# A linear-attention phase of a fused transformer kernel: a new step order, a three-pass output projection, and q's squares on another engine

## The reference

```
q, k, v = silu(x@Wq), silu(x@Wk), silu(x@Wv)          # 16 heads x 64
g = sigmoid(x@Wf - dt_bias); beta = sigmoid(x@Wb); A = exp(-exp(A_log))
q, k = q/|q|, k/|k|
for t:  o_t = (q_t . state) * g_t
        state = A*state + beta_t * k_t (x) v_t
o = o * rsqrt(mean(o*o) + 1e-5) * norm_w * sigmoid(x@Wg + bg)
y = o @ Wo                                            # 1024 -> 128
```

## Time and profile before

| | us |
|---|---|
| median of 3 runs | 917.35 (914.67 to 918.21) |
| the profiled execution | 915.93 |
| its span | 913.8 |

### The profile page before, as it was taken

The page is one execution under the profiler, slowest core; times in us unless marked ns, Lnnn a source line. Parts: engine busy times, 40 slices in busy tenths (PEclk is TensorE's granted clock), DMA queues, the critical chain, the costliest instruction groups (busy, mean ns, idle before and its releaser), DMA issues. The chain is left out here.

```text
span 913.8 us, 31013 instructions
## 1 busy us (share of the span) xinstructions
PE 841.7 (92%) x13152; PEld 717.5 (79%) x13152; DVE 548.9 (60%) x1247; ACT 511.6 (56%) x1105; POOL 636.4 (70%) x530
## 2 busy tenths in 40 slices
PE   4858998999797789999999999999999999998897
PEld 3648998899695678887888888888888888877786
DVE  3986566566684455655655655656556556666563
ACT  4745553565566636645646556566466467364354
POOL 3973211321455988898898898898898898988352
PEclk9998999999997889999999999999999999999999
DMA  5001000100100000000000000000000000000011
GB/s 189 25 13 34 25 12 1 31 19 1 25 1 1 1 3 3 3 3 3 3 3 2 3 4 2 3 4 2 3 3 3 4 2 3 4 1 3 3 36 57
DMA packets 19415, 12.36 MB, mean 14 GB/s; under 512 B 7760, under 2 KB 18768, under 8 KB 19024
## 3 DMA queue, kind: packets, MB, share of 16 engines
q1 hardware_dynamic: 19280, 10.39, 3.9%
HBM read 8.29 MB, written 2.10 MB: 11 GB/s over the span
## 5 line engine op out<-in xcount | busy, mean ns | idle before, releaser
L2101 POOL TENSOR_TENSOR la_scale<-la_scale,lt_mhalf 128x32 f32<-128x32 f32 x16 | 100.6, 6285 | 43.4 <-DVE la_scale L1756 43.4
L1446 PE MATMUL la_ps<-la_x_hi,w_hi 128*128 128x256 f32 x384 | 120.2, 313 | 0.4 <-ACT la_v L1897 0.4
L1447 PE MATMUL la_ps<-la_x_lo,w_hi 128*128 128x256 f32 x384 | 108.2, 282 | 0.0
L1448 PE MATMUL la_ps<-la_x_hi,w_lo 128*128 128x256 f32 x384 | 108.1, 281 | 0.0
L2061 POOL TENSOR_TENSOR la_coef<-la_ssk,lt_mhalf 128x32 f32<-128x32 f32 x16 | 87.0, 5440 | 13.8 <-DVE la_ssk L1774 13.8
L1797 DVE TENSOR_TENSOR lt_state<-la_s_ps,la_faded 128x512 f32<-128x512 f32 x62 | 42.3, 682 | 71.9 <-PE la_o_ps L1525 48.6
L1446 PEld LDWEIGHTS la_ps<-la_x_hi,w_hi 128*128 128x128 f32 x384 | 72.9, 190 | 16.0 <-issue 7.4
L531 POOL CAST at_q_hi<-qk_hi 128x128 fp32r<-128x128 f32 x32 | 9.4, 294 | 106.1 <-PE at_s_ps L572 103.6
L598 PE MATMUL at_o_ps<-V,at_probsT 128*128 128x128 f32 x544 | 75.1, 278 | 3.2 <-DVE at_probsT L507 2.0
L2079 POOL TENSOR_TENSOR la_k<-la_k,lt_decay_k 128x1024 f32<-128x1024 f32 x32 | 75.6, 2364 | 2.1 <-ACT n_xn L1953 2.1
L2086 POOL TENSOR_TENSOR la_qdT<-la_qT,lt_decay_q 128x1024 f32<-128x1024 f32 x32 | 76.3, 2384 | 0.0
(11 more groups left out here) (207 smaller groups left out, 2382.6 us busy)
## 6 DMA issues: line engine op xcount, KB each, us to landing
at_w_raw<-in_w SPq DMA_DIRECT2D x20, 128.0 KB, 2.2
X<-in_x SPq DMA_DIRECT2D x8, 256.0 KB, 2.9
out<-X SPq DMA_DIRECT2D x8, 256.0 KB, 2.3
qkv_cos<-in_cos SPq DMA_DIRECT2D x1, 1024.0 KB, 4.8
qkv_sin<-in_sin SPq DMA_DIRECT2D x1, 1024.0 KB, 7.0
lt_w_out<-in_w_out SPq DMA_DIRECT2D x4, 128.0 KB, 2.7
const<-in_const SPq DMA_DIRECT2D x1, 320.5 KB, 3.2
qkv_w<-in_w_qkv SPq DMA_DIRECT2D x1, 320.0 KB, 3.9
```

Of the source, the lines that this page charges most:

```text
L1446: eng.matmul(out, l_hi, r_hi, start=True, stop=False)
L1447: eng.matmul(out, l_hi, r_lo, start=False, stop=False)
L1448: return eng.matmul(out, l_lo, r_hi, start=False, stop=True)
L2101: eng.tensor_tensor(scale[:, :, :], scale[:, :, :], powers, ALU.pow).then_inc(s["scale_step"], 1)
```

## The change

- **Order.** Every engine's step is rearranged. On TensorE the whole-array products are put together, and the quarter-array work between them stands in five groups: su; then attend, turn_k, attend, recall; scores, sq, recall, update; attend, turn_k, attend, recall; scores, recall, update. The scores of the first sequence are made one step earlier (`scored`), as is `fade(m, 0, 0)`. `turn_scales` and the b jobs come after the first update, `project_out` after q3.
- **Projection.** ScalarE copies u to a high part (`high_u`), VectorE makes the low part (`low_u`), and `project_out` runs three fp32r products for each of 8 chunks. The weights are split once, in the lead-in. To make room, u_hi and u_lo lie on the memory of sq and gate and the weights' low part on that of w_out, with waits added for it.
- **q's squares** go from VectorE to ScalarE (`square_q`), and **one of two `decay_queries`** from GpSimd to VectorE.

```diff
-def make_room(self, sb):
+def make_room(self, nc, sb):
+    with ExitStack() as whole:
+        self.w_out = whole.enter_context(nc.sbuf_tensor("lt_w_out", [P, NP, P], F32))
+    self.w_out_lo = sb("lt_w_out_lo", [P, NP, P], F32R)
+    self.w_out_hi = sb("lt_w_out_hi", [P, NP, P], F32R)
...
 faded = sb("faded", [P, B, NP, D])
 u = sb("u", [P, NP, W])
-sq = sb("sq", [P, NP, W])
+with ExitStack() as before_scaling:
+    sq = before_scaling.enter_context(nc.sbuf_tensor("la_sq", [P, NP, W], F32))
+    gate = before_scaling.enter_context(nc.sbuf_tensor("la_gate", [P, NP, W], F32))
+u_hi = sb("u_hi", [P, NP, W], F32R)
+u_lo = sb("u_lo", [P, NP, W], F32R)
...
-        return exists(m + 1) if job != "sq" else exists(m)
+    if job in ("be", "s00", "s01") or job[0] in "kqv":
+        return exists(m + 1)
     return exists(m)
 STEPS = range(-2, NT + 1)
 LAST = NT - 1
-ring = Ring(("f0 be s00 s01 f1 su k0 f2 sT k1 f3 v0 kT0 kT1 sq g0 k2 g1 k3 g2 sB g3 v1 b0 b1 b2 b3 v2 y s10 s11 "
-             "v3 yt xt q0 q1 kT2 kT3 q2 q3").split(), has, STEPS, BANKS)
+ring = Ring(("f0 f1 su f2 sT f3 be k0 k1 v0 v1 kT0 kT1 k2 k3 s10 s11 sq sB b0 b1 b2 b3 v2 v3 q0 q1 q2 q3 y g0 g1 yt g2 "
+             "kT2 kT3 g3 xt s00 s01").split(), has, STEPS, BANKS)
+def scored(m, b):
+    return m - 1 if b == 0 else m
 def free(eng, m, job):
...
-    for job in ("kT2", "kT3", "q3"):
-        taken(eng, m - 1, job)
-banks = [free(eng, m, f"s{b}{odd}") for odd in range(2)]
+for job in ("kT2", "kT3") if b else ("kT0", "kT1", "q3"):
...
-    for j in range(4):
-        taken(eng, m, f"b{j}")
+    if m == 1:
+        eng.wait_ge(s["w_lo_ready"], 1)
+    eng.wait_ge(s["ulo_ready"], 4 * m)
     bank = free(eng, m, "y")
+    out = ps[bank][:, 0:W]
     for c in range(NP):
-        mm = eng.matmul(ps[bank][:, 0:W], w_out[:, c, :], u[:, c, :], start=(c == 0), stop=(c == NP - 1))
+        eng.matmul(out, tables.w_out_hi[:, c, :], u_hi[:, c, :], start=(c == 0), stop=False)
+        eng.matmul(out, tables.w_out_hi[:, c, :], u_lo[:, c, :], start=False, stop=False)
+        mm = eng.matmul(out, tables.w_out_lo[:, c, :], u_hi[:, c, :], start=False, stop=(c == NP - 1))
     mm.then_inc(full[bank], 1)
 def turn_y(m):
...
     prv, now, nxt = exists(m - 1), exists(m), exists(m + 1)
     if now:
         by_feature(m, "f0")
-    if nxt:
-        betas(m + 1)
-    if now:
-        scores(m, 0)
-    if now:
         by_feature(m, "f1")
     if prv:
         sum_squares(m, "su")
-    if nxt:
-        by_token(m, "k0")
     if now:
         by_feature(m, "f2")
     if prv:
         turn_totals(m)
-    if nxt:
-        by_token(m, "k1")
     if now:
         by_feature(m, "f3")
     if nxt:
+        betas(m + 1)
+        by_token(m, "k0")
+        by_token(m, "k1")
         by_token(m, "v0")
-        turn_k(m, 0)
-    if now:
-        sum_squares(m, "sq")
-        by_feature(m, "g0")
-    if nxt:
-        by_token(m, "k2")
-    if now:
-        by_feature(m, "g1")
-    if nxt:
-        by_token(m, "k3")
-    if now:
-        by_feature(m, "g2")
-    if prv:
-        turn_scales(m)
-    if now:
-        by_feature(m, "g3")
-    if nxt:
         by_token(m, "v1")
-    if prv:
-        for j in range(4):
-            spread_scales(m, j)
     if now:
         attend(m, 0, 0)
     if nxt:
-        by_token(m, "v2")
+        turn_k(m, 0)
     if now:
         attend(m, 0, 1)
-    if m == 0:
-        update((m, 0, 0))
-    if prv:
-        project_out(m)
+        recall(m, 0, 0)
+    if nxt:
+        by_token(m, "k2")
+        by_token(m, "k3")
     if now:
-        recall(m, 0, 0)
         scores(m, 1)
-    if nxt:
-        by_token(m, "v3")
-    if prv:
-        turn_y(m)
-    if m == LAST:
-        eng.wait_ge(up_read[1], B * LAST)
-        ffn.turn(eng, 0)
-    if exists(m + 2):
-        turn_x(m + 2)
-    if now:
+        sum_squares(m, "sq")
         recall(m, 0, 1)
     if now and nxt:
         update((m, 0, 1), (m, 1, 0))
     elif now:
         update((m, 1, 0))
+    if prv:
+        turn_scales(m)
+        for j in range(4):
+            spread_scales(m, j)
+    if m == LAST:
+        eng.wait_ge(up_read[1], B * LAST)
+        ffn.turn(eng, 0)
     if nxt:
-        by_feature(m, "q0")
-        by_feature(m, "q1")
+        by_token(m, "v2")
+        by_token(m, "v3")
+        for j in range(4):
+            by_feature(m, f"q{j}")
+    if prv:
+        project_out(m)
     if now:
+        by_feature(m, "g0")
+        by_feature(m, "g1")
+    if prv:
+        turn_y(m)
+    if now:
+        by_feature(m, "g2")
         attend(m, 1, 0)
     if nxt:
         turn_k(m, 1)
     if now:
         attend(m, 1, 1)
+        recall(m, 1, 0)
+        by_feature(m, "g3")
+    if exists(m + 2):
+        turn_x(m + 2)
+    if nxt:
+        scores(m + 1, 0)
     if m == LAST:
         ffn.turn(eng, 1)
-    if nxt:
-        by_feature(m, "q2")
-    if now:
-        recall(m, 1, 0)
-    if nxt:
-        by_feature(m, "q3")
     if now:
         recall(m, 1, 1)
     if now and nxt:
         update((m, 1, 1), (m + 1, 0, 0))
+    elif nxt:
+        update((0, 0, 0))
 for m in STEPS[:-1]:
     step(m)
...
 eng.wait_ge(s["u_ready"], 2 * B * NT)
 ffn.receptance(eng, 0)
 ffn.keys(eng, 1)
+turn_scales(NT)
 ffn.values(eng, 0)
 ffn.receptance(eng, 1)
-ffn.turn(eng, 3)
-turn_scales(NT)
-ffn.values(eng, 1)
 for j in range(4):
     spread_scales(NT, j)
+ffn.turn(eng, 3)
 ffn.keys(eng, 2)
 ffn.receptance(eng, 2)
 project_out(NT)
+ffn.values(eng, 1)
 ffn.values(eng, 2)
 turn_y(NT)
 ffn.receptance(eng, 3)
...
+        bank = written(eng, scored(m, b), f"s{b}{odd}")
         eng.tensor_tensor(pT[:, odd::2, :], ps[bank][:, :].rearrange("p (r t) -> p r t", r=NP), decay[:, odd::2, :],
                           ALU.mult).then_inc(read[bank], 1)
-def square_q(m):
-    taken(eng, m - 1, "q3")
-    for part in (slice(0, 4), slice(4, 8)):
-        eng.tensor_tensor(sq[:, part, :], qT[:, part, :], qT[:, part, :], ALU.mult).then_inc(s["qsq_ready"], 1)
 def guard_q(m):
     bank = written(eng, m, "sq")
...
     part = u[:, 2 * j:2 * j + 2, :]
     eng.tensor_tensor(part, two(bank), part, ALU.mult).then_inc(read[bank], 1)
+def low_u(m, j):
+    eng.wait_ge(s["uhi_ready"], 4 * (m - 1) + j + 1)
+    part = slice(2 * j, 2 * j + 2)
+    eng.tensor_tensor(u_lo[:, part, :], u[:, part, :], u_hi[:, part, :].bitcast(F32), ALU.subtract).then_inc(s["ulo_ready"], 1)
 def sum_k(n, b):
     eng.wait_ge(s["ksq_ready"], B * n + b + 1)
...
 if b == 0 and m > 0:
-    written(eng, m, "y")
+    eng.wait_ge(s["ulo_ready"], 4 * m)
 for odd in range(2):
     part = slice(odd * NP // 2, (odd + 1) * NP // 2)
...
         new_state(m - 1, 1, 1)
     if prv:
         add_totals(m)
+        gather_totals(m)
+        gate_u(m - 1, 0)
         gate_u(m - 1, 1)
-        gather_totals(m)
     if now:
-        square_q(m)
+        decay_queries(eng, m, 1)
     if now and exists(m + 2):
         normalize(m + 2)
-    if now:
-        guard_q(m)
     if m == LAST:
         ffn.moments(eng, 2)
         ffn.moments(eng, 3)
+    if now:
+        new_state(m, 0, 0)
+        decayed(m, 1)
+        guard_q(m)
     if nxt:
         sum_k(m + 1, 0)
+        sum_k(m + 1, 1)
+        guard_k(m + 1)
+    if now and nxt:
+        new_state(m, 0, 1)
     if prv:
         for j in range(4):
             scale_u(m, j)
-    if nxt:
-        sum_k(m + 1, 1)
-        guard_k(m + 1)
+        for j in range(4):
+            low_u(m, j)
     if m == LAST - 1:
         ffn.normalize(eng, 0)
         ffn.normalize(eng, 1)
     if now:
-        new_state(m, 0, 0)
-        decayed(m, 1)
         gate_o(m, 0)
-    if prv:
-        residual(m)
-    if now and nxt:
-        new_state(m, 0, 1)
-    if now:
-        gate_u(m, 0)
     if m >= -1 and exists(m + 3):
         norm.moments(eng, Tile(0, m + 3))
     if m == LAST - 2:
         ffn.moments(eng, 0)
+        ffn.moments(eng, 1)
+    if prv:
+        residual(m)
+    if m == LAST:
+        ffn.normalize(eng, 2)
     if now:
         new_state(m, 1, 0)
         gate_o(m, 1)
-    if m == LAST - 2:
-        ffn.moments(eng, 1)
+    if m == -1:
+        split_w_out()
 for m in STEPS[:-1]:
     step(m)
-ffn.normalize(eng, 2)
+gate_u(LAST, 0)
 add_totals(NT)
 gate_u(LAST, 1)
 gather_totals(NT)
 ffn.normalize(eng, 3)
+scale_u(NT, 0)
+scale_u(NT, 1)
+low_u(NT, 0)
+scale_u(NT, 2)
+low_u(NT, 1)
+scale_u(NT, 3)
+low_u(NT, 2)
+low_u(NT, 3)
 ffn.output(eng, 0)
 ffn.moments(eng, 4)
-for j in range(4):
-    scale_u(NT, j)
 ffn.output(eng, 1)
 ffn.normalize(eng, 4)
 ffn.moments(eng, 5)
...
         eng.wait_ge(s["ug_ready"], B * m)
+        written(eng, m, "y")
 bank = written(eng, m, f"{kind}{j}")
 for r in range(2):
...
+def high_u(m, j):
+    taken(eng, m, f"b{j}")
+    if j == 0 and exists(m):
+        written(eng, m, "sq")
+    part = slice(2 * j, 2 * j + 2)
+    eng.activation(u_hi[:, part, :], u[:, part, :], ACT.Copy).then_inc(s["uhi_ready"], 1)
+def high_w_out():
+    eng.wait_ge(tables.w_ready, 1)
```

(95 more changed lines are left out.)

45 lines of the change are left out of this document (27 added, 18 removed).

## The result

| | before | after |
|---|---|---|
| median, us | 916.01 (914.5 to 918.21, 4 runs) | 974.25 (973.3 to 976.72, 4 runs) |
| span of the profiled execution | 913.8 | 971.3 |
| mean granted TensorE clock | 0.976 | 0.944 |

The changed kernel is slower by 6.4%: ratio 1.0638, 95% interval 1.0605 to 1.0671. The forecast of 940 had the sign, but 974 lies outside its range of 905 to 956.

What follows compares the result with a forecast made beforehand. The prediction took TensorE to bound the linear phase, busy 39.75 of 40 us. From 915.9 it summed +22.4 (fourteen steps), +6 (clock) and -4 - 1 - 1 + 1 (ends) to 939.3, forecast as 940, range 905 to 956.

Steps and rivals of the forecast that it cites:

- The stall: TensorE waiting for VectorE's chain once a step: 3.05 us, 0.55 before job b0 and 2.5 before v2.
- TensorE's own savings: Shorter projection, fewer array-shape changes, no wait before the last recall, less new self-waits: 1.43 us saved a step.
- self-wait behind attend: recall(b,0) right behind attend(b,1) waits for its end: 0.25 us each, two a step, 0.50 lost.
- The step with the clock up: One step of the linear phase without clock falls: 34.9 - 1.43 + 3.05 = 36.5 us.
- The clock: TensorE's clock falling to half behind the new stall, about 1.7 us each, in one step in four: +6 us.
- the clock falls in every step: Rival: half clock behind the stall in every step, +18 us more than forecast, 958; chance 12%.
- The ends: Start, last step and tail outside the steady steps: -4, -1, -1 and +1 us, each possibly off by 2.
- Start: f0 of step 1 comes earlier, fades and keys being ahead in GpSimd's queue: -4, and -1 for step 1.
- Last step: The last step of the linear phase, which waits for the power either way: -1 us.
- Tail: After the last step, scale_u and low_u ahead of the projection and ffn.output(0) later: +1 us in all.
- The rule of exclusive use: VectorE's gates and query decay would wait for GpSimd's power: 3 us more a step, some 980; chance 3 in 100.
- TensorE stays the bound: Rival: VectorE's chain is shorter than read, no stall, up to 1.43 us gained a step, about 893; chance 18%.

Runs made afterwards that it cites:

- b0: Changed kernel with VectorE's scale_u and low_u moved ahead of the second key sum, guard_k and new_state(m,0,1): 938.7 us, ratio 1.0264 (the job b0 is something else).
- b2: b1 plus turn_scales(m) ahead of scores(m,1) on TensorE and copy_scales ahead of square_k(0) on ScalarE: 925.54 us, ratio 1.0126.
- e1: d1 with GpSimd's inverse roots of the next norm behind fade(m,1,0), and VectorE's normalize behind new_state(m,0,1): 911.99 us, ratio 0.9953.
- a2: Changed kernel with the products of job b3 made eight times over in steps 1 to 14, useless work filling the stall: 952.69 us, ratio 1.0402.
- a1: Changed kernel with only VectorE's scale_u moved ahead of the second key sum, low_u left behind: 971.18 us, ratio 1.0602.
- e2: e1 with the output projection in plain fp32 as before, without high_u and low_u: 921.71 us, ratio 1.0067.
- a4: Changed kernel with the queues behind the last step (turn_scales, spread scales, VectorE's and ScalarE's scale work) in the order of before: 964.97 us, ratio 1.0544.
- d1: c2 with VectorE's second key sum and guard_k behind low_u again, only the first key sum still ahead: 915.63 us, ratio 1.0001.
- b1: b0 plus, on GpSimd, the coefficients and the first weigh_v ahead of fade(m+1,0,0): 926.34 us, ratio 1.0122.
- b3: b2 plus the edits of a4: 919.88 us, ratio 1.0045 (the job b3 is something else).
- d2: d1 with the products of job b3 made twelve times over in the last step, useless work: 916.39 us, ratio 1.0013.
- c2: b3 with sum_k(0) ahead of decayed(m,1), sum_k(1) and guard_k ahead of scale_u, and last-step decay_keys(m,1) ahead of GpSimd's power: 922.96 us, ratio 1.0088.

## Why the prediction was wrong

Point by point, by its own steps.

- *The stall: right in place, cause and size.* Forecast 0.55 before b0 and 2.5 before v2; measured 0.47 and 2.39. b0 shows the cause: with VectorE's two groups exchanged it is gone.
- *TensorE's own savings: right.* The projection takes 479.29 to 482.17 = 2.88 us (forecast 2.82, 3.65). The self-wait behind attend is 463.07 - 462.29 = 0.78 against 0.51: 0.27, forecast 0.25. TensorE's floor was forecast as 33.5; the unhindered steps of b2 take 33.3 and those of e1 33.7.
- *The step with the clock up: right.* Forecast 36.5; the only step without a fall took 36.66, and the steps of a2 36.78.
- **The clock: the first step that failed.** "I take one step in four: +6." Of the twelve steps measured, eleven had half the clock right behind the stall (granted 0.95 or 0.96 over eight of the steps, 0.91 or 0.92 over three), and this cost 1.76 a step against 0.43 forecast. The fourteen steps grew by 45.8 instead of 28.4, so this term was 17.4 us too small. The rival "the clock falls in every step" had the right mechanism, and its +18 is what the term needed. The prediction had the one row that bore on it, a wait of 2.44 us with half the clock behind it, and a new wait of the same length; it weighed that row at one in four because there was only one. a2 confirms the size by filling the gaps and changing nothing else: -21.6. That one row did not say "every step" either: in a1 a wait of 2.6 us at another place brought the clock down in seven steps of thirteen. How often was open, and what decides it is not shown.
- **The ends: the second step that failed.** Forecast -5 at the start and nothing at the end; measured -0.3 and +12.0, together 16.7 us off. *Start:* "fades and keys come ahead in GpSimd's queue; -4". TensorE's wait for x_lo went, and one for GpSimd's weigh_v took its place:

```profile
305.57 1.97 PE L1558 MATMUL la_s_ps<-la_v,la_k 64*64 64x64 f32 x32 [4.70 <-POOL la_v L2120]
```

  *Last step:* forecast -1, measured +3.6. Without v and q projections nothing stands between the b banks and the projection, so the waits that the steady step hides come out. Two rows of that step (after), and 15 us of it by stretch, with the clock at 0.54:

```profile
889.42 1.70 PE L1558 MATMUL la_s_ps<-la_v,la_k 64*64 64x64 f32 x32 [1.84 <-POOL la_k L2128]
...
898.05 0.58 PE L1609 MATMUL la_ps<-la_u_hi,lt_w_out_hi 128*128 128x256 f32 x1 [2.92 <-DVE la_u_lo L1770]
```

```profile
889.00:904.00 15.00, 11.19 (x76) 10.27 (x77) 6.17 (x10) 4.35 (x9) 5.44 (x8) 0.54 0.00 1
```

  At that clock the new projection takes 903.34 - 898.05 = 5.3 us. It has a part in the loss: in e1 and e2 the last step takes 29.5 us with it and 26.5 without.

  *Tail:* forecast +1, measured +8.4. The prediction counted the operations that were put ahead on VectorE and missed that turn_scales was put ahead of values(0) and receptance(1) in TensorE's queue, where it holds both for 3.8 us until GpSimd's power is done. a4 takes 7.0 of it away. Every wait that a new order makes ends in one of the queues, the prediction says itself; this queue it did not lay out.
- *The rule of exclusive use: its consequence rightly refused, half of it overlooked.* After, as before, VectorE's gates (two inputs of 1024 elements) ran beside the power in 2.41 us for two, so VectorE did not wait for the power's end and the 980 of that rival fell with it. But the prediction looked at VectorE's side alone. The 6.34 us are not the power's undisturbed time. In the tail, with no such operation beside it, the same instruction takes 5.46:

```profile
457.29 2.41 DVE L1796 SCALAR_TENSOR_TENSOR la_u<-la_gate,la_u 128x1024 f32<-128x1024 f32 x2
457.45 6.34 POOL L2142 TENSOR_TENSOR la_scale<-la_scale,lt_mhalf 128x32 f32<-128x32 f32 x1 [1.31 <-DVE la_scale L1757]
...
915.57 5.46 POOL L2142 TENSOR_TENSOR la_scale<-la_scale,lt_mhalf 128x32 f32<-128x32 f32 x1 [3.20 <-DVE la_scale L1757]
```

  At 457.45 the first gate half has 1.05 us to go, and 1.05 + 5.29 = 6.34; where 0.61 of a VectorE operation is left (345.40, after) the power takes 5.89. GpSimd waits for the VectorE operation that is already running. The other way it happens as well: in the kernel before, one half of the gates (L1789, 580.34) took 1.83 us and not 1.21 while GpSimd's weigh_v ran until 581.09. The Trainium skill ("SBUF — State Buffer", section "Who interferes with whom") has a VectorE operation with two SBUF inputs and a GpSimd operation that reads SBUF exclude each other, and these rows agree with it; only a VectorE operation that starts while the power runs is not held. That cost the forecast nothing, since it took the measured 6.34, but it is why d1's power is late in its three longest steps, which e1 took away.
- *The rival "TensorE stays the bound"* (893) was wrong for this order of VectorE's queue. Of the 58 us lost, b0 (VectorE's chain) gave back 35.6, b1 (GpSimd's order) 12.4 and the tail 5.7 in b3. Each repair showed the next queue to be close behind. Once VectorE's chain was gone GpSimd's came out at 1 to 1.4 us a step, and e1, with that gone too, still has 34.46 and not 33.7.

The two misses, 17.4 and 16.7, are the 34 us between the forecast's span and the measured one.

Left open: the short gaps in e1's steps (below); the old step order with the three-pass projection alone, which no run tried; and the last step, where d2 lifted half of the clock's fall without a gain.

## What to carry to other kernels

A new wait of the engine that bounds a phase is priced with the clock that it costs: where the trace has one row of a wait as long as the new one, with half the clock behind it, give "in every step" a large chance (eleven of twelve here, seven of thirteen in a1) and put the price of both ends into the range. The duration of a GpSimd operation that always runs beside the same VectorE operation is not its own: look for one row where it runs alone. A steady step's cover (here six projection blocks between the scales and the product that needs their low parts) is absent in the first and last steps, so lay those two out by hand as well, and the tail's queues with them. When three engines are each within 1 to 2 us of a 35 us step, moving one chain only names the next; follow the wait from engine to engine until the one that sets the step waits for nothing. And split the number of an experiment by steps and ends: e2's 9.7 us hide 19.4 in twelve steps one way and 9.9 at the end the other way.

## What the runs showed of the hardware

- Waits of TensorE of 2.4 us once a step had half the clock behind them in eleven of twelve steps. Waits of 2.6 us in a1 had it in seven of thirteen. The waits of 0.3 to 1.4 us in c2 at the place of the first, 15.0 us in all, left the clock up until 826 us, in the middle of step 14:

```profile
342.00:826.00 484.00, 456.12 (x9701) 394.16 (x9703) 290.97 (x523) 327.98 (x636) 390.10 (x251) 1.00 0.01 3
```

  And making the idle time busy with useless products was worth 21.6 us (a2).
- GpSimd and VectorE hold each other up where a VectorE operation has both inputs in SBUF (d1, before and after, above): GpSimd's two inverse roots took 1.19 + 1.56 us beside the gates and 0.19 + 0.70 alone, the power 6.34 and 5.46.
- In e1 six of the twelve steps take 34.7 to 36.1 us and the others 33.7 to 34.0, at the same clock, with the same counts of instructions. Two thirds of the difference sit in gaps, most of them in the middle of 32 or 64 quarter-array products, where the profile shows nothing that was waited for:

```profile
491.00 0.93 PE L1558 MATMUL la_s_ps<-la_v,la_k 64*64 64x64 f32 x48 [0.92 <-issue]
```

  It is not explained. e1 has eleven such gaps of 0.25 to 0.92 us between 342 and 792, 7.2 us in all.
